# One step list for the last batch of cross-attention, the causal attention and the last layer of a two-layer perceiver kernel; causal products in plain float32

## The reference, cut to what matters

```python
# L1_xattn: 16 heads of 32; softmax(q k^T / sqrt(32)) v over the 1601 context rows of the batch
q, k, v = x @ Wq.T, y @ Wk.T, y @ Wv.T
out = softmax(SCALE * q k^T) v;  return out @ Wp.T + bp
# L1_attn: the same within the 64 tokens of a batch, causal (the window of 128 never cuts)
q, k, v = x @ Wq.T, x @ Wk.T, x @ Wv.T
y = softmax(q k^T * scale + mask) v;  return y @ Wo.T
# L1_ffn: rows quantised to int8 by their own maximum, integer weights
x_scale = max(|x|)/127;  x_q = clip(round(x / x_scale));  out = (x_q @ wq.T) * x_scale * ws + bias
```

## Time and profile before

| | |
|---|---|
| three runs | 1291.32, 1292.21, 1295.77 us, median 1292.21 |
| the profiled execution, device time | 1284.61 us |
| its span, first to last instruction | 1282.8 us |
| mean granted TensorE clock | 0.952 of full |
| PE busy | 1153.2 us (90%) |
| DVE, ACT, POOL busy | 634.2 (49%), 426.2 (33%), 338.9 us (26%) |

### The profile page before, as it was taken

The page is one execution under the profiler, slowest core; times in us unless marked ns, Lnnn a source line. Parts: engine busy times, 40 slices in busy tenths (PEclk is TensorE's granted clock), DMA queues, the critical chain, the costliest instruction groups (busy, mean ns, idle before and its releaser), DMA issues.

```text
span 1282.8 us, 34101 instructions
## 1 busy us (share of the span) xinstructions
PE 1153.2 (90%) x15663; PEld 864.1 (67%) x15664; DVE 634.2 (49%) x977; ACT 426.2 (33%) x806; POOL 338.9 (26%) x366
## 2 busy tenths in 40 slices
PE   6888979796999999999999999999999999654986
PEld 3343434385788888887888887888887887442863
DVE  2011368546214555555555555556555545555286
ACT  1010152214224334334434434434334334221332
POOL 0000000104001333333333333233233233349122
PEclk9999989799999999999999999999999999766999
DMA  9999970633012002001002002002001003100000
GB/s 352 373 397 352 378 282 0 225 106 108 1 38 67 19 23 67 18 23 67 18 23 68 19 23 67 18 23 68 18 23 56 30 23 120 56 2 17 1 2 33
DMA packets 38879, 115.67 MB, mean 90 GB/s; under 512 B 2504, under 2 KB 3016, under 8 KB 34640
## 3 DMA queue, kind: packets, MB, share of 16 engines
q1 hardware_dynamic: 38736, 113.50, 24.6%
HBM read 112.44 MB, written 1.05 MB: 88 GB/s over the span
## 4 chain that ended last, share of the span: by engine, by line
PE 75%; DVE 8%; ACT 5%; SPq 5%; DMA 4%; issue 2%; POOL 0%; DVEq 0%; POOLq 0%; ACTq 0%
PE SB L389 45%; PE SC L1099 6%; PE SB L380 5%; PE SB L1129 4%; SPq L546 4%; DMA R<-in_ctx_t 2%; PE SB L925 2%; PE SC L1108 2%; ACT R L1615 1%; DMA R<-in_ctx 1%; PE SC L1092 1%; DVE LN L746 1%; PE SB L993 1%; PE SC L901 1%; PE SB L981 1%
## 5 line engine op out<-in xcount | busy, mean ns | idle before, releaser
L1615 ACT COPY R<-SB 64x512 f32<-64x512 f32 (+1 forms) x224 | 116.3, 519 | 202.0 <-PE SB L389 200.2
L1414 DVE TENSOR_REDUCE LN<-SC 128x64 f32<-128x768 f32 x128 | 116.6, 952 | 131.4 <-PE SC L1099 131.4
L389 PE MATMUL SB<-high,whigh 128*128 128x512 f32 (+2 forms) x512 | 180.3, 352 | 1.0 <-ACT Z L402 1.0
L389 PE MATMUL SB<-high,wlow 128*128 128x512 f32 (+2 forms) x512 | 178.8, 349 | 0.0
L389 PE MATMUL SB<-low,whigh 128*128 128x512 f32 (+2 forms) x512 | 177.3, 346 | 0.0
L389 PE MATMUL SB<-wlow,high 128*128 128x512 f32 (+1 forms) x416 | 167.5, 403 | 0.0
L389 PE MATMUL SB<-whigh,high 128*128 128x512 f32 (+1 forms) x416 | 165.3, 397 | 0.0
L389 PE MATMUL SB<-whigh,low 128*128 128x512 f32 (+1 forms) x416 | 165.2, 397 | 0.0
L686 POOL TENSOR_TENSOR added<-LN 128x768 f32<-128x768 f32 x32 | 58.6, 1831 | 285.4 <-ACT LN L1647 285.4
L686 POOL TENSOR_TENSOR added<-Z 128x768 f32<-128x768 f32 x32 | 58.7, 1833 | 273.5 <-ACT Z L1647 273.5
L1642 ACT COPY LN<-SC 128x128 f32<-128x128 f32 x64 | 17.0, 266 | 271.6 <-PE SC L1108 271.3
(11 more groups left out here) (224 smaller groups left out, 1872.3 us busy)
## 6 DMA issues: line engine op xcount, KB each, us to landing
R<-in_ctx_t SPq DMA_DIRECT2D x32, 1024.0 KB, 8.5
R<-in_ctx SPq DMA_DIRECT2D x8, 3072.0 KB
R<-in_ctx_t SPq DMA_DIRECT2D x16, 644.0 KB, 7.0
R<-in_f SPq DMA_DIRECT2D x4, 2048.0 KB, 15.4
R<-in_f SPq DMA_DIRECT2D x1, 8192.0 KB, 26.2
R<-in_ctx_t SPq DMA_DIRECT2D x12, 512.0 KB, 3.6
R<-in_Wk SPq DMA_DIRECT2D x3, 1024.0 KB, 11.0
R<-in_Wv SPq DMA_DIRECT2D x3, 1024.0 KB, 13.2
```

Of the source, the lines that this page charges most:

```text
L389: last = pe.matmul(out_, lhs[a][:, k, :], rhs[b][:, k, :], start=n == 0, stop=n == 3 * NC - 1)
L1414: inc(dve.tensor_reduce(tops[:, r * T:(r + 1) * T], sc_head[:, :, r, 0:6 * T].rearrange("p g (a q) -> p q g a", q=T), AX.XY, ALU.max), "ha ...
L1615: last = act.copy(keys[nu][64 * half:64 * half + 64, pairs, first * P:first * P + full], src[:, :, 0:full])
```

## The change

All of batches 0 to 6 stays as it is. `LAST4` becomes a list written out, of some 280 steps, that holds the attention steps of batch 7 and everything behind them; DVE, ACT and POOL walk it too, each doing its steps in its order. New steps: `R` norm of a tile for the causal attention, `n` its transposes, `Q`, `K` causal queries and keys in two groups of columns (group 0: tiles 0 to 2, 384 columns; group 1: tile 3, 128 columns), `V` values of a tile, then by batch `S` scores, `E` exponential, `U` sum, `T` transposes, `P` times values, `O` transposes, by tile `Y` output product, `N` norm and quantising, `A` rounding, `X` transposes, `W` last product, `C` cast of the last weights, `0` a memset on POOL, and `r` the reading of a job's bank by the engine that `reader` names. All jobs use the three banks of the ring. The order of the whole list:

```diff
-LAST4 = attention(LATE4 + [("y", 0), ("y", 1), ("y", 2)], ahead=False, ends=True)
+LAST4 = [
+    ("0", 0), ("p", (("w", 10), 7)),
+    ("s", 0), ("o", -1), ("w", 10), ("p", (("w", 11), 9)), ("m", 0), ("w", 11), ("b", 0), ("p", (("w", 12), 1)),
+    ("z", -1), ("e", 0), ("w", 12),
+    ("s", 1), ("0", 1), ("y", 0), ("m", 1), ("r", ("y", 0)), ("b", 1), ("R", 0), ("e", 1), ("y", 2), ("r", ("y", 2)),
+    ("s", 2), ("0", 2), ("n", 0), ("y", 1), ("r", ("n", 0)), ("R", 2), ("m", 2), ("r", ("y", 1)), ("o", 0), ("n", 2),
+    ("R", 1), ("b", 2), ("V", 0), ("n", 1), ("r", ("n", 2)), ("r", ("n", 1)),
+    ("s", 3), ("Q", (0, 0)), ("m", 3), ("r", ("V", 0)), ("z", 0), ("b", 3), ("K", (0, 2)), ("e", 2),
+    ("r", ("Q", (0, 0))),
+    ("s", 4), ("e", 3), ("r", ("K", (0, 2))), ("V", 1), ("m", 4), ("o", 1), ("b", 4), ("r", ("V", 1)), ("Q", (0, 2)),
+    ("s", 5), ("K", (0, 3)), ("r", ("Q", (0, 2))), ("r", ("K", (0, 3))), ("m", 5), ("Q", (0, 1)), ("b", 5),
+    ("K", (0, 0)), ("z", 1), ("e", 4),
+    ("s", 6), ("Q", (0, 3)), ("r", ("K", (0, 0))), ("r", ("Q", (0, 1))), ("e", 5), ("m", 6), ("o", 2), ("b", 6),
+    ("K", (0, 1)), ("r", ("Q", (0, 3))), ("r", ("K", (0, 1))),
+    ("s", 7), ("S", 0), ("z", 2), ("e", 6), ("S", 1), ("m", 7), ("r", ("S", 0)), ("b", 7), ("e", 7), ("E", 0),
+    ("r", ("S", 1)), ("U", 0), ("V", 2), ("r", ("V", 2)), ("T", 0), ("r", ("T", 0)), ("E", 1), ("S", 2), ("o", 3),
+    ("r", ("S", 2)), ("z", 3), ("P", 0), ("T", 1), ("r", ("P", 0)), ("y", 3), ("U", 1), ("r", ("T", 1)), ("E", 2),
...
+    ("P", 5), ("r", ("S", 7)), ("V", 3), ("Y", 0), ("E", 6), ("r", ("P", 5)), ("E", 7), ("U", 6), ("U", 7),
+    ("r", ("V", 3)), ("T", 6), ("O", 4), ("r", ("Y", 0)), ("r", ("T", 6)), ("P", 6), ("O", 5), ("r", ("O", 4)),
+    ("r", ("P", 6)), ("N", 0), ("Y", 1), ("r", ("O", 5)), ("T", 7), ("r", ("T", 7)), ("r", ("Y", 1)), ("P", 7),
+    ("O", 6), ("r", ("P", 7)), ("A", 0), ("Y", 2), ("N", 1), ("O", 7), ("r", ("Y", 2)), ("r", ("O", 6)), ("X", 0),
+    ("r", ("O", 7)), ("r", ("X", 0)), ("Y", 3), ("N", 2), ("A", 1), ("r", ("Y", 3)), ("X", 1), ("A", 2), ("X", 2),
+    ("r", ("X", 1)), ("W", 0), ("W", 1), ("N", 3), ("r", ("W", 0)), ("r", ("X", 2)), ("r", ("W", 1)), ("A", 3),
+    ("W", 2), ("X", 3), ("r", ("X", 3)), ("r", ("W", 2)), ("W", 3), ("r", ("W", 3))
+]
```

The lines left out hold the causal batches 2 to 5, the norm of tile 3 (`R`, `n`), and the eight products of group 1. The products lose the three passes and their splits (`dhigh`, `dlow`, `norm4_low` and the POOL work on them go):

```diff
+                    elif kind in "QK":
+                        group, ec = x
+                        pe.wait_ge(sem("d0_in" if kind == "Q" else "d1_in"), 16)
+                        for tt in range(3) if group == 0 else (3,):
+                            read_of("n", tt)
+                        at_, weight, bk = columns5(group), dt["QK".index(kind)], bank4(job)
+                        for k in range(NC):
+                            last = pe.matmul(bk[:, 0:at_.stop - at_.start], weight[:, k, ec * P:(ec + 1) * P],
+                                             LT[:, k, at_], start=k == 0, stop=k == NC - 1)
+                        done4(job, last)
```

Loads on SP's queue:

```diff
+            sp.wait_ge(sem("s4"), HP * (B - 1))
+            inc(sp.dma_start(wp4, natural(Wp4)), "wp4_in", 16)
+            inc(sp.dma_start(dt[0], natural(Wq5)), "d0_in", 16)
+            inc(sp.dma_start(dt[1], natural(Wk5)), "d1_in", 16)
             sp.wait_ge(sem("pv4"), 4 * (B - 1))
-            inc(sp.dma_start(wp4, natural(Wp4)), "wp4_in", 16)
-            for w, wt in enumerate((Wq5, Wk5, Wv5, Wo5)):
-                inc(sp.dma_start(dt[w], natural(wt)), f"d{w}_in", 16)
+            inc(sp.dma_start(dt[2], natural(Wv5)), "d2_in", 16)
+            inc(sp.dma_start(dt[3], natural(Wo5)), "d3_in", 16)
             inc(sp.dma_start(wq32, natural(wq)), "wq_in", 16)
 
-            sp.wait_ge(*filled("y4", 3))
+            sp.wait_ge(sem("pv4"), 4 * B)
```

POOL zeroes the query tile in two parts and the value tile between them; before, it zeroed the query tile, split three weights and zeroed the value tile:

```diff
+            for kind, x in LAST4:
+                if kind == "e":
+                    sums_of(B - 1, x)
+                elif kind == "0" and x == 0:
+                    for job in [j for j in BATCH4[B - 2] if j[0] == "k"][-RING4:]:
+                        n, k = before_last[job]
+                        pool.wait_ge(sem(f"full4_{n}"), before + k + 1)
+                    inc(pool.memset(qb5[:, 0:4], 0.0), "zero5")
+                elif kind == "0":
+                    for late in LATE4:
+                        n, k = at[late]
+                        pool.wait_ge(sem(f"full4_{n}"), at4(LAST4, B - 1)[1] + k + 1)
+                    inc(pool.memset(v5, 0.0) if x == 1 else pool.memset(qb5[:, 4:6], 0.0), "zero5")
+                elif kind == "r" and x[0] == "S":
...
+                    inc(pool.tensor_tensor(v, v, mx5[:, b % 2, :].unsqueeze(2).to_broadcast([P, HP, T]),
+                                           ALU.subtract), "sub5")
```

More of the change, by code:

```diff
@@ L229, in mid_jobs @@
     add("q4", 4, "da")
[L230 to L243, removed]
     return jobs
@@ L681, in _ @@
             inc(pool.nop(), "sums4", 2)
-            for b in range(B):
-                for pr in range(HP):
[L684 to L712, removed]
@@ L810, in rounded, with columns5 @@
             inc(act.activation(xq[:, tt, :], xq[:, tt, :], ACT.Identity, bias=minus_round[:, 0:1]), "xq")
[L812 to L823, removed]
+        def columns5(group):
+            return slice(0, 3 * P) if group == 0 else slice(3 * P, 4 * P)
@@ new lines, in read_out5 @@
+        def read_out5(eng, me, job, bk):
+            kind, x = job
+            copy = eng.tensor_copy if me == "d" else eng.copy
+            if kind == "n":
+                return copy(LT[:, :, x * P:(x + 1) * P], b4(bk))
+            if kind == "Q":
+                group, ec = x
+                slots = slice(0, 6) if group == 0 else slice(0, 2)
+                for j in range(4):
+                    rows = slice(32 * j, 32 * j + 32)
+                    last = copy(qb5[rows, slots, 2 * ec + j // 2, (j % 2) * T:(j % 2 + 1) * T],
+                                bk[rows, 0:T * (slots.stop)].rearrange("p (b t) -> p b t", t=T))
+                return last
+            if kind == "K":
+                group, ec = x
+                at = columns5(group)
+                return copy(k5[:, ec, at], bk[:, 0:at.stop - at.start])
+            if kind == "V":
+                for w in range(2):
+                    src = bk[w * T:(w + 1) * T, :].rearrange("p (j n) -> p j n", n=P)
+                    for s_ in range(2):
+                        last = copy(v5[s_ * T:(s_ + 1) * T, 2 * x + w, :, s_ * 64:(s_ + 1) * 64],
+                                    src[:, :, s_ * 64:(s_ + 1) * 64])
+                return last
+            if kind == "T":
+                return copy(pt5[:, x % 2, :], bk[:, :])
+            if kind == "O":
+                return copy(ot[:, :, x * T:(x + 1) * T], bk[:, 0:256].rearrange("p (k q) -> p k q", q=T))
+            if kind == "X":
+                return copy(xqt[:, :, x * P:(x + 1) * P], b4(bk))
@@ L1449, in _ @@
-            steps4(dve, run4)
-            dve.wait_ge(sem("xbp"), 4)
-            for tt in range(NT - 1):
-                norm_rows(dve, 4, tt)
-            for tt in range(NT - 1):
-                norm_low(dve, 4, tt, norm4_low)
-            norm(dve, 4, add_row("y4"), tiles=range(NT - 1, NT))
-            norm_low(dve, 4, NT - 1, norm4_low)
-            dve.wait_ge(sem("zero5"), 2)
-            queries_out(dve, "d")
-            evacuate(dve, "d", "k5", lambda i: (k5[:, i, :], bank("k5", i)[:, :]))
@@ L1474, in masked @@
+            def masked(b, bk, read, done):
+                v = by_pair(p5[:, b % 2, :])
+                if b == 0:
+                    dve.wait_ge(sem("causal"), 3)
+                dve.scalar_tensor_tensor(out=v, in0=by_pair(bk[:, :]), scalar=HEAD_SCALE,
+                                         in1=causal[:, :].unsqueeze(1).to_broadcast([P, HP, T]),
+                                         op0=ALU.mult, op1=ALU.add).then_inc(read, 1)
+                dve.wait_ge(read, done)
                 if b >= 2:
@@ L1513, in scales @@
                 dve.wait_ge(sem("xqa"), tt + 1)
                 inc(dve.tensor_scalar(xq[:, tt, :], xq[:, tt, :], 127.0, ROUND, ALU.min, ALU.add), "xqb")
[L1516 to L1527 removed]
+            steps4(dve, run4)
@@ L1647, in run4 @@
                             inc(act.activation(part, part, ACT.Exp, scale=HEAD_SCALE), "e4")
+                    elif kind == "R":
+                        norm_sqrt(act, 4, x)
+                    elif kind == "N":
+                        norm_sqrt(act, 5, x)
+                    elif kind == "E":
+                        act.wait_ge(sem("sub5"), x + 1)
+                        inc(act.activation(p5[:, x % 2, :], p5[:, x % 2, :], ACT.Exp), "e5")
+                    elif kind == "A":
+                        rounded(act, x)
+                    elif kind == "r" and reader(*x) == "a":
+                        n, k = at[x]
+                        act.wait_ge(sem(f"full4_{n}"), before + k + 1)
+                        if x[0] in "QV":
+                            act.wait_ge(sem("zero5"), 3)
```

(1 more changed line is left out.)

404 lines of the change are left out of this document (202 added, 202 removed), and 8 rows, old and new, of the table LAST4.

## The result

The changed kernel takes 1229.44 us (median of four runs, 1225.5 to 1231.14) against 1291.76 for the kernel before (four runs, 1285.67 to 1295.77). The ratio is 0.9508, with a 95% interval of 0.947 to 0.9545: 62.3 us off.

The account below looks back on a forecast made before the run. PE was taken to bound the kernel, idle and slow in batch 7. Pairs of 62.0 us, 67 behind them and the tail ended at 1228.4 against 1282.8; less 2 for the port, 52.4 off: 1232.2, plus 7.6, forecast 1240, range 1227 to 1259.

Parts of the forecast that it names:

- What bounds: Whole kernel: PE holds nearly all the time, except near the end, where batch 7 leaves it idle at low clock.
- The pairs: Batch 7, pairs 1 to 7 walked with filling: 62.0 us, only 4.8 us gained by itself.
- Prices: PE at full clock: plain products 3.43, 2.57 and 1.17 us by columns; causal products 43.6 us against 35.6.
- Behind pair 7: From pair 7's spread to the last Y: 61.1 us of PE work, 67 with waits and hand-offs.
- the 2 us for hand-offs: Behind pair 7: an allowance of 2 us added to the 3.6 us of waits walked step by step.
- 0.4 that DVE is late: Tail from the addition of tile 3: the old 12.8 us plus 0.4 us for DVE's lateness.
- Tables: ACT's Sqrt and Exp loads: seven instead of three, 1.28 us each, between 0 and 5.1 us, taken as 0.
- The port: DVE norm rows beside POOL operations, on a shared port: 0 to 13 us over seven rows, taken as 2.
- the median of the three runs shown is 7.6 above it, so I forecast 1240: Whole kernel: 7.6 us between profiled execution and median, carried from the profiled forecast of 1232.2 to 1240.
- not beside its work: POOL's memset and splits and the norm's splitting, called beside PE's wait for the norm, not beside PE's work.
- The filling of batch 7: First rival, pairs 2 to 7: filling adds itself to the bare chain, 21 us later, 1261; chance 0.09.
- the second rival: Causal part behind pair 7 bound by its hops, PE idle and its clock falling: 15 us more, 1255; chance 0.19.

Follow-up runs that it names:

- plain_only: Kernel before with q5, v5, k5 as plain float32 products without norm_low and splits, order untouched: 1293.45 us, ratio 1.0033.
- staged_tail: Changed kernel up to the spread of pair 7, then outputs, products, causal batches and last layer stage after stage: 1251.90 us, ratio 0.9701.
- port: Changed kernel with POOL's memset of the value tile held back to run beside tile 0's norm rows on DVE: 1230.44 us.
- tail_order: Changed kernel with Y 0 and N 0 earlier, group 1 query copies on ACT, and T, P, O and X 0 moved: 1235.78 us, ratio 0.9584.
- no_fill: Changed kernel with the list sorted, batch 7's attention steps first and all other steps behind them: 1277.98 us, ratio 0.9896.

## Why the prediction was right, and where it was off

- *What bounds.* Right: the idle time of PE in batch 7, at half clock, is what went. Emptying the pairs again brings back 49 us, some 5 of them for another reason, where the change took off 57.
- *The pairs.* 62.0 us were walked from the first scores of pair 1 to the spread of pair 7, and 63.75 measured; the first six sum to 57.2 walked and 58.5 measured. Each was within 0.5.
- *Prices.* The 384-column product, which no row showed, was 2.57 by proportion, and the chain shows 2.58 (row below), or 2.78 behind a pair's scores. Plain products: 8 us more of PE work was said; `plain_only`, where every product has all 512 columns, shows 7.6.

```profile
1132.88 2.58 PE SB L1237 x8
```

- *Behind pair 7.* From the first scores of pair 1 to the addition of tile 3 the walk had 129.4 with the 2 us for hand-offs in it; it measured 127.0. The allowance was needed: from the spread of pair 7 to the end of `Y` 3 PE is idle 6.5 of 62.9 us, against the 3.6 + 2 of the walk. What was too high is the work, 61.1 against 56.4 busy. The prices were read where PE had stood idle before; back to back the same steps are shorter. `P` was taken as 1.17 and a transpose as 0.66, and the chain has the rows below; the eight products of group 1 were taken as 9.4 and are one piece of 7.30 in `staged_tail`. From 1207.33 to the last rounding the chain is DVE's, the norms of tiles 1 to 3 in a row, and PE waits for it once (0.52 us ahead of `Y` 3). The "0.4 that DVE is late" is what the rows show, 1215.79 to 1216.19.

```profile
1187.61 0.89 PE SB L1272 x8
1188.50 0.44 PE SB L1264 x4
```

- *Tables.* Taken as 0, right: seven loads, as said, each 1.28 and hidden. By the Trainium skill (ScalarE: Activation LUTs, What ACT_TABLE_LOAD costs) a switch has another 1.38 us of drain; the rows show 0.02 between load and activation, so the measurement decides.
- *The port.* 2 us were allowed, 0.1 occurred (one row of 0.64). The price is real, as the `port` run shows, but the order happens to keep clear of it; that part is luck. By the Trainium skill (SBUF — State Buffer, Who interferes with whom) the loser blocks for the whole instruction, and the trace agrees: 2.52 in place of 0.55, until the memset had ended.
- *The largest miss* is "the median of the three runs shown is 7.6 above it, so I forecast 1240". I carried this difference over as if it lay outside the change. None of it carried over: the changed kernel's profile is 1.1 above its own median. A part lay in what the change removes, the race of the norm rows of tile 3 against POOL's splits and memset, won in the profile; taking it away alone lowers the median of the kernel before by 5.0 (2.5 to 8.7 by the interval). A part was chance in three runs: all 68 executions of the kernel before on record have their median at 1288.9, 4.3 above the profiled one and not 7.6.
- *The 10.6 us in all*, from the forecast down: 7.6 for this difference and 0.2 of rounding; 4.5 by which S is shorter than the 154.9 of the sum (pairs 1.7 longer, the stretch behind them 4.1 shorter, the tail 0.2 shorter, the 2 us for the port not used); 1.1 between profile and median; less 2.9, as batch 7 began later in this execution. That the sum for the profiled execution, 1232.2, comes within 2 us of the 1230.53 measured is thus partly luck: the late begin of batch 7 hides 2.9 of the 4.5.
- I also wrote of the splits that they stood beside PE's wait, "not beside its work", and costed their removal at nothing of its own. They made that wait: 4.26, 1.92 and 4.53 us of rows that take 0.55. `plain_only` shows that the splits account for only 2.3 us of it and the memsets for the rest. As the sum rebuilt the whole stretch, that part was in it; the race was not.
- *The rivals.* The filling of batch 7 did lie beside the chain, and behind pair 7 the clock stayed at 1.00 although PE waited for hops. `tail_order` shows what the second rival looks like when it comes true: 0.74 and 5 us.

## What to carry to other kernels

A serial chain at the end of a long, full kernel costs twice, by the waits and by PE's clock, and work from behind it pays for being cut up even at a dearer price per product. When the profiled execution is well off the median, look for what differs before carrying the difference through a sum: rows next to each other on two engines that begin within a microsecond are a race, and a second profile shows it; then ask what sets each side, which here was PE's clock. Take the price of a step from rows in which the engine came straight from other work, if the stretch will be filled; the others were too high here. In a merged list count what stands at the head of each in-order queue, not only each engine's work.

## What was not expected of the hardware

- A DVE row that waits for POOL's port can be passed by the next POOL operation as well: due at 1182.20, it waited for a subtraction that ended at 1185.69 and for the memset behind it until 1189.14. The wait is then 6.9 us though no single operation is over 4.6. In the `port` run a row took 2.48 us in the same way, beside a sum of 0.45 and a memset of 1.80.
- The clock stood at its lower level, 0.50, over 26 us of `no_fill` in which PE was busy 13.21 us, and at 1.00 over the 11.60 us behind pair 7 of the changed kernel, in which PE was busy 9.35.
- The same kernel's clock rises at different times: one product of eight records took 4.41 us in one execution and 5.76 in another, and by the race behind it the causal products began 6.8 us later.
